# Attention probabilities as two fp16 halves, turned by DMA transposes instead of on TensorE

## The reference

```python
xn = ln(layernorm(x))                                  # per batch: 128 x 512
q, qx = ln(fp8(xn) @ wq.T), ln(fp8(xn) @ wqx.T)        # 16 heads each, d = 128
k, v = ln(fp8(xn) @ wk.T), fp8(xn) @ wv.T              # 8 groups, 2 heads share one
kx, vx = ln(cond @ w_kv_x[:1024].T), cond @ w_kv_x[1024:].T
def gqa(q, k, v):
    p = softmax(q @ k.T / sqrt(128))                   # 128 x 128 for each head
    return p @ v
cat = concat([gqa(q, k, v), gqa(qx, kx, vx)])          # 32 heads
x = x + fp8(cat / smooth) @ wproj.T * scale
```

## Time and profile before

| | |
|---|---|
| median of 3 runs | 3359.56 us (3355.34 to 3360.89) |
| the profiled execution | 3357.83 us |
| its span | 3356.0 us |
| mean granted TensorE clock | 0.948 of full |
| first residual written (L642) | at 194.7 us |
| last residual written | at 1156.4 us |

### The profile page before, as it was taken

One profiled execution on the slowest core, in us unless ns is written; L12 is line 12 of the kernel. 1 busy time (PEld: TensorE's weight loads), 2 busy tenths in 40 slices (PEclk: granted clock), 3 DMA queues, 4 the chain that ended last, 5 costly groups with the idle time before them and its releaser, 6 DMA issues. The chain is left out here.

```text
span 3356.0 us, 58815 instructions
## 1 busy us (share of the span) xinstructions
PE 2983.1 (89%) x17284; PEld 1767.7 (53%) x17285; DVE 1847.9 (55%) x5780; ACT 1650.6 (49%) x4374; POOL 1684.7 (50%) x2331
## 2 busy tenths in 40 slices
PE   4699999999999789999999995999999999734996
PEld 2366666666666545555555542555555555422663
DVE  4366666656665564434443363778878877421331
ACT  5577777777777533332333242555555555311332
POOL 6477667766776345534544453544444444241222
PEclk8799999999999989999999997999999999856998
DMA  7601101110110155544554473000000000217444
GB/s 239 216 30 42 38 28 35 41 38 28 35 44 29 67 178 156 152 134 138 154 155 140 129 221 68 17 26 19 19 25 19 19 25 14 65 74 273 85 83 105
DMA packets 202977, 285.48 MB, mean 85 GB/s; under 512 B 38721, under 2 KB 109633, under 8 KB 202817
## 3 DMA queue, kind: packets, MB, share of 16 engines
q1 hardware_dynamic: 140016, 204.89, 18.8%
q0 software_dynamic: 16640, 38.05, 5.6%
q10 hardware_dynamic: 46224, 41.36, 4.2%
HBM read 194.95 MB, written 93.50 MB: 86 GB/s over the span
## 5 line engine op out<-in xcount | busy, mean ns | idle before, releaser
L437 PE MATMUL a_mm<-a_w_hi,a_xq_hi 128*128 128x512 f16 x768 | 298.4, 389 | 64.0 <-POOL a_xq_lo L885 60.9
L601 DVE BATCH_NORM_STATS2 a_st<-a_mm 128x6 f32<-128x128 f32 x768 | 170.8, 285 | 318.8 <-PE a_mm L438 225.3
L750 ACT ACTIVATE a_nrm<-a_mm,a_sc_t 128x128 f32<-128x128 f32 x768 | 290.5, 473 | 105.9 <-POOL a_sc_t L903 105.7
L1646 POOL TENSOR_TENSOR e_st<-e_st,e_ws_tile 128x1024 f32<-128x1024 f32 x64 | 124.5, 1946 | 428.3 <-PE e_y L1402 417.5
L438 PE MATMUL a_mm<-a_w_hi,a_xq_lo 128*128 128x512 f16 x768 | 298.4, 389 | 0.0
L1535 DVE SCALAR_TENSOR_TENSOR e_hl<-e_ha,e_hh 128x512 f16<-128x512 f32 x128 | 88.5, 691 | 352.0 <-ACT e_hh L1440 351.6
L1440 ACT ACTIVATE e_hh<-e_ha 128x512 f16<-128x512 f32 x128 | 76.3, 596 | 415.3 <-PE e_ha L1387 413.7
L902 POOL TENSOR_TENSOR a_sc_t<-a_sc_t,a_mhalf 128x4 f32<-128x4 f32 x192 | 199.9, 1041 | 133.1 <-DVE a_sc_t L608 132.7
L1401 PE MATMUL e_y<-e_w2l,e_hh 128*128 128x512 f16 x640 | 242.9, 380 | 0.0
L1402 PE MATMUL e_y<-e_w2h,e_hl 128*128 128x512 f16 x640 | 242.9, 380 | 0.0
L1400 PE MATMUL e_y<-e_w2h,e_hh 128*128 128x512 f16 x640 | 242.9, 380 | 0.0
(11 more groups left out here) (357 smaller groups left out, 8653.7 us busy)
## 6 DMA issues: line engine op xcount, KB each, us to landing
e_st<-in_w SPq DMA_DIRECT2D x128, 512.0 KB, 4.1
disp<-a_empty SPq DMA_DIRECT2D x16, 781.5 KB, 4.1
e_st<-in_w1b SPq DMA_DIRECT2D x32, 352.0 KB, 3.1
e_xb<-disp ACTq DMA_DIRECT2D x41, 260.5 KB, 2.7
disp<-a_empty SPq DMA_DIRECT2D x4, 2605.0 KB, 21.5
e_xb<-disp SPq DMA_DIRECT2D x40, 260.5 KB, 4.3
a_cx<-in_ctxT SPq DMA_DIRECT2D x32, 256.0 KB, 3.1
a_stage<-in_wprojT SPq DMA_DIRECT2D x16, 512.0 KB, 5.0
```

What stands on the lines that cost most here:

```text
L437: pe.matmul(out, xq_hi[:, n, c, :], w_hi[:, t, c, :], start=(c == 0), stop=False)
L750: ins = act.activation(nrm[:, n % 2, i * P:(i + 1) * P], src[:, i * P:(i + 1) * P], ACT.Identity, bias=sc_t[:, n % 2, 3, i:i + 1], scale=s ...
```

## The change

Probabilities and values are kept as two fp16 parts each (high and low). ACT writes the high part of the probabilities, times PS = 1024, and DVE the rest; SP turns both with DMA transposes (128x512 each) into `pT`, and the value product is three fp16 products (high x high, high x low, low x high) in place of one in fp32. The values are split by ACT (`v_keep`) and DVE (`v_low`). `p_transpose` and `p_keep` are gone, `pv` and `out_project` come one slot later, `o_quant`, `final`, `store` and all `r_*` stages too, and the waits of the other users of PTB are changed accordingly. The factor PS is taken out in `rsm`.

```diff
-        vt = s.sb("vt", [P, 4, DM], F32)
+        vt = [s.sb(f"v{n}", [P, 4, DM], F16) for n in ("h", "l")]
         pr = s.sb("pr", [P, 2, DM], F32)
-        pT = s.sb("pT", [P, 2, DM], F32)
+        pq = [s.sb(f"pq{n}", [P, 2, DM], F16) for n in ("h", "l")]
+        pT = [s.sb(f"p{n}", [P, 2, DM], F16) for n in ("h", "l")]
...
+            def p_turn(b, a):                                         # SP
+                for half, done in ((0, "p_hi"), (1, "p_lo")):
+                    sp.wait_ge(sem[done], at(a, NA, b))
+                    if half == 0 and not (isinstance(b, int) and b == 0 and a < 2):
+                        sp.sem_inc(sem["turning"], 1)
+                        sp.wait_ge(sem["pv"], at(a - 2, NA, b))
+                    sp.sem_inc(sem["turning"], 1)
+                    sp.dma_start_transpose(pT[half][:, a % 2, :].rearrange("p (i t) -> p i t", t=P),
+                                           pq[half][:, a % 2, :]).then_inc(turned[half][a % 2], 16)
-            run_pipeline(sp, [("job", 0, ... weights ...), ("att", 5, residual), ("end", 10, store), ("in", 1, x_load)],
+            run_pipeline(sp, [("job", 0, ... weights ...), ("att", 4, p_turn), ("att", 5, residual),
+                              ("end", 11, store), ("in", 1, x_load)],
...
             def pv(b, a):                                             # PE
-                pe.wait_ge(sem["p_ok"], at(a, NA, b))
+                for half in range(2):
+                    pe.wait_ge(turned[half][a % 2], 16 * at(a // 2, NA // 2, b))
...
                 for i in range(2):
-                    mm = pe.matmul(OVB[:, i * 256:(i + 1) * 256], vt[...], pT[...], start=True, stop=True)
+                    pe.matmul(OVB[:, two], vh, ph, start=True, stop=False)
+                    pe.matmul(OVB[:, two], vh, pl, start=False, stop=False)
+                    mm = pe.matmul(OVB[:, two], vl, ph, start=False, stop=True)
-                              ("att", 3, p_transpose), ("att", 5, pv), ("att", 9, out_project), ("in", 6, x_transpose)],
+                              ("att", 6, pv), ("att", 10, out_project), ("in", 6, x_transpose)],
...
+            def v_low(b, t):                                          # DVE, waits for v_hi
+                    dve.scalar_tensor_tensor(out=vt[1][:, i, :], in0=MMB[BANK[t]][:], scalar=scal[:, col:col + 1],
+                                             in1=vt[0][:, i, :], op0=ALU.mult, op1=ALU.subtract).then_inc(sem["v_ok"], 1)
+            def p_low(b, a):
+                dve.wait_ge(sem["p_hi"], at(a, NA, b))
+                if not (isinstance(b, int) and b == 0 and a < 2):
+                    dve.wait_ge(turned[1][a % 2], 16 * at(a // 2 - 1, NA // 2, b))
+                dve.scalar_tensor_tensor(out=pq[1][:, a % 2, :], in0=pr[:, a % 2, :], scalar=PS, in1=pq[0][:, a % 2, :],
+                                         op0=ALU.mult, op1=ALU.subtract).then_inc(sem["p_lo"], 1)
-            run_pipeline(dve, [("att", 2, row_scale), ("att", 1, smax), ("att", 6, o_quant), ("end", 10, final), ("end", 10, r_stats),
-                               x_quants, ("job", 0, stats), ("job", 0, convert), ("in", 3, x_stats), ...
+            run_pipeline(dve, [("att", 2, row_scale), ("att", 1, smax), ("att", 3, p_low), ("att", 7, o_quant),
+                               ("end", 11, final), ("end", 11, r_stats),
+                               x_quants, ("job", 0, stats), ("job", 1, v_low), ("job", 0, convert), ("in", 3, x_stats), ...
...
             def exps(b, a):                                           # ACT
-                    act.wait_ge(sem["ptr"], at(a - 2, NA, b))
+                    act.wait_ge(sem["p_lo"], at(a - 2, NA, b))
-            def p_keep(b, a):
-                act.wait_ge(sem["ptr"], at(a, NA, b))
+            def p_high(b, a):
+                act.wait_ge(sem["pnorm"], at(a, NA, b))
                 if not (isinstance(b, int) and b == 0 and a < 2):
-                    act.wait_ge(sem["pv"], at(a - 2, NA, b))
-                act.activation(pT[:, a % 2, :], PTB[:], ACT.Copy).then_inc(sem["p_ok"], 1)
+                    act.wait_ge(turned[0][a % 2], 16 * at(a // 2 - 1, NA // 2, b))
+                act.activation(pq[0][:, a % 2, :], pr[:, a % 2, :], ACT.Copy, scale=PS).then_inc(sem["p_hi"], 1)
                ..., ("job", 3, q_keep), ("att", 1, exps), ("job", 1, normalise), ("job", 0, convert),
-                               ("att", 3, p_keep), ("job", 1, v_keep), ...
+                               ("att", 3, p_high), ("job", 1, v_keep), ...
```

More of the change, by code:

```diff
@@ L270, in layer0_attention @@
             "x_in", "c_in", "x_stat", "x_scal", "x_norm", "x_tr", "x_t", "y_act", "y_pool", "xq", "xq_ok", "cx_hi", "cx_lo",
-            "mm", "stat", "scal", "norm", "v_ok", "qtr", "q_ok",
-            "score", "max", "exp", "rinv", "pnorm", "ptr", "p_ok", "pv", "oy", "cq", "proj",
+            "mm", "stat", "scal", "norm", "v_hi", "v_ok", "qtr", "q_ok",
+            "score", "max", "exp", "rinv", "pnorm", "p_hi", "p_lo", "turning", "pv", "oy", "cq", "proj",
             "xres", "x1", "out", "filled", "disp_filled", "rconst", "r_stat", "r_scal", "r_norm", "r_tr", "r_t",
             "r_lgt", "r_lg", "r_max", "r_exp", "r_mask", "r_px", "r_pos", "r_slot")}
+        turned = [[s.sem(f"turned_{n}{i}") for i in range(2)] for n in ("h", "l")]
         staged = [s.sem(f"staged{i}") for i in range(NSTAGE + LENT)]
@@ L389, in store @@
                                  empty[:].unsqueeze(1).to_broadcast([P, FILL, RW])).then_inc(sem["filled"], 16)
-            run_pipeline(sp, [("job", 0, lambda b, t: weights(b, t + 1)), ("att", 5, residual), ("end", 10, store), ("in", 1, x_load)],
+            def p_turn(b, a):
[7 more added lines that the diff above has]
+                                           pq[half][:, a % 2, :]).then_inc(turned[half][a % 2], 16)
+            run_pipeline(sp, [("job", 0, lambda b, t: weights(b, t + 1)), ("att", 4, p_turn), ("att", 5, residual),
+                              ("end", 11, store), ("in", 1, x_load)],
                          NJ, SCORE_AT, head=HEAD)
@@ L401, in x_transpose @@
                 pe.wait_ge(sem["x_norm"], b + 1)
[L402 to L405, removed]
+                if isinstance(b, int) and b == 0:
                     pe.wait_ge(sem["small"], 16 * N_SMALL)
+                if not (isinstance(b, int) and b < 3):
+                    pe.wait_ge(sem["r_lg"], b - 2)
                 for c in range(KT):
@@ L461, in scores @@
                 mm.then_inc(sem["score"], 1)
[L463 to L479, removed]
             def pv(b, a):
@@ L487, in pv @@
                 for i in range(2):
-                    g = 2 * (a % 2) + i
-                    mm = pe.matmul(OVB[:, i * 256:(i + 1) * 256], vt[:, KV_OF[a], g * P:(g + 1) * P],
-                                   pT[:, a % 2, i * 256:(i + 1) * 256], start=True, stop=True)
+                    g, two = 2 * (a % 2) + i, slice(i * 256, (i + 1) * 256)
+                    vh, vl = (v[:, KV_OF[a], g * P:(g + 1) * P] for v in vt)
+                    ph, pl = (p[:, a % 2, two] for p in pT)
+                    pe.matmul(OVB[:, two], vh, ph, start=True, stop=False)
+                    pe.matmul(OVB[:, two], vh, pl, start=False, stop=False)
+                    mm = pe.matmul(OVB[:, two], vl, ph, start=False, stop=True)
                 mm.then_inc(sem["pv"], 1)
@@ L504, in out_project @@
                 mm.then_inc(sem["proj"], 1)
[L506 to L508 removed]
             def r_transpose(b, k):
[L511 to L512 removed]
+                if not (isinstance(b, int) and b == 0):
                     pe.wait_ge(sem["r_pos"], b)
@@ L690, in x_quant_of @@
                 return lambda b, k: x_quant(b, n)
-            run_pipeline(dve, [("att", 2, row_scale), ("att", 1, smax), ("att", 6, o_quant), ("end", 10, final), ("end", 10, r_stats),
-                               *(("in", at_, x_quant_of(n)) for n, at_ in enumerate(X_QUANT_AT)), ("job", 0, stats),
-                               ("job", 0, convert), ("in", 3, x_stats), ("end", 16, r_scores), ("end", 18, r_pick),
-                               ("end", 20, r_slots)], NJ, SCORE_AT, ch, head=HEAD)
+            run_pipeline(dve, [("att", 2, row_scale), ("att", 1, smax), ("att", 3, p_low), ("att", 7, o_quant),
+                               ("end", 11, final), ("end", 11, r_stats),
+                               *(("in", at_, x_quant_of(n)) for n, at_ in enumerate(X_QUANT_AT)), ("job", 0, stats), ("job", 1, v_low),
+                               ("job", 0, convert), ("in", 3, x_stats), ("end", 17, r_scores), ("end", 19, r_pick),
+                               ("end", 21, r_slots)], NJ, SCORE_AT, ch, head=HEAD)
         @block.scalar
@@ L817, in _ @@
                                ("in", 9, convert_at(-1)), ("job", 3, q_keep), ("att", 1, exps), ("job", 1, normalise), ("job", 0, convert),
-                               ("att", 3, p_keep), ("job", 1, v_keep), ("in", 4, x_norm), ("in", 6, x_back),
```

(7 more changed lines are left out.)

15 lines of the change are left out of this document (9 added, 6 removed).

## The result

| | before | after |
|---|---|---|
| median | 3357.45 us (3354.96 to 3360.89, 4 runs) | 3786.16 us (3784.7 to 3791.99, 4 runs) |
| ratio | | 1.1279, interval 1.126 to 1.1299 |
| profiled execution, its span | 3357.83, 3356.0 | 3791.99, 3790.2 |
| mean granted TensorE clock | 0.948 | 0.911 |

What follows compares the result with a forecast made beforehand. PE bounds the kernel before; a new loop of waits across DVE, POOL and ACT would bound it after. Batch 0 41 + 14 x 26.7 + drain 10 = 425 us on 3357.8: forecast 3785 us, range 3560 to 4000.

Steps and rivals of the forecast that it cites:

- The ring: First attention: p_low, stats, scales, normalise, exps, p_high wait in a circle; turns of 8.45 and 10.14 us plus extras; chance 0.72.
- PE's 5.2 us a batch are worth nothing: First attention: PE loses 0.65 us a head, 5.2 a batch, 83 in all, which become idle time.
- The ring's extras of slots 3 and 0: POOL's work ahead of scales: x_scale makes slot 3's turn grow by 5.3 us; pnorm, ctx_low, r_scale and others add 5.1 in slot 0.
- A batch of 93.7: First attention's batch after the change: 74.4 us of turns plus 19.3 of other work on the loop, 5.86 a slot.
- Batch 0, +41: First residual at 236 us against 194.7: p_turn(3) behind the fills, free at 160, then 13 slots, 76 us.
- A batch of 67.0 before: First attention in the kernel before: 14 batches from 193 to 1131 us, 67.0 us each, 4.19 a slot.
- The drain, +10: After the last slot 15: turns of 4.5 us without projections, 36 us against 26.
- The transposes, 1.6 us each, hidden: SP's 256 DMA transposes of 128 KB: 1.6 us each taken, two per turn hidden up to 5.9 us each.
- The rival in which they bind: Transposes take over from 5.9 us each; at 8 us, 128 us a batch and 4263 in all; chance 0.12.
- DVE's wait of 2 to 4 us at p_low: Sign in the profile after: DVE's longest wait is for ACT's p_high at p_low, 2 to 4 us, 120 times.
- PE at 65%: Sign in the profile after: PE's busy share in the first attention falls from 96% to near 65%.

Runs made afterwards that it cites:

- p_low_last: Kernel after with p_low moved behind stats and v_low of its slot in DVE's queue: 3431.73 us, ratio 1.0225.
- p_low_twice: Kernel after with DVE doing p_low twice in each step: 3877.9 us, ratio 1.156.
- pv_twice: Kernel after with PE making the six value products of each step twice: 3793.82 us, ratio 1.1307.
- fill_spread: Kernel after with the four 2605 KB fills issued one by one behind the transposes of steps 4 to 7 of batch 0: 3765.81 us.
- turn_twice: Kernel after with each transpose issued twice from batch 1 on, the first time into unused memory: 3797.16 us, ratio 1.1319.
- p_high_first: Kernel after with p_high moved ahead of exps and normalise of its slot in ACT's queue: 3573.03 us, ratio 1.0647.
- all_moves: Kernel after with p_low last, p_high first, x_scale, x_norm, ctx_low and r_scale later, and batch 0's big fills spread: 3288.54 us.

## Why the prediction was right, and where it was off

Point by point, by its own steps:

- **The ring** (chance 0.72): right, and shown from both sides. Order alone takes back 354 us (p_low_last); work in the ring costs its full length (p_low_twice), work beside it a tenth (pv_twice). Seven of the eight turns agree with their sums to 0.5 us.
- **PE's 5.2 us a batch are worth nothing**: right as a term (0.65 us a step, as summed), and right that it becomes idle time.
- **The ring's extras of slots 3 and 0**: right. Moving their pieces gave 107 us where these terms gave 114.
- **A batch of 93.7**: the mean over the 14 was 94.3, but two errors partly cancel in it. In the loop a batch takes 95.17, because one turn of eight has a `p_low` of 2.28 us in place of 0.69 (below). And the last batch prepares no next one: its turns lack x_scale, y_part and the rest, and it takes 1320.0-13x95.17 = 83 us. I had given it 93.7 like the others.
- **Batch 0, +41**: 43.9, and along the path described: SP issued the transpose behind the fills at 144.64, where it took the queue 10.36 us; PE stood still for it until 162.52 (160 forecast); from there to the first residual it is 76.1 us (76 forecast). What the change adds here is mostly the ring's slower slots and not the fills, which delay the kernel before by about as much (fill_spread, p_low_last).
- **A batch of 67.0 before**: half a microsecond too long. The kernel before writes its residual in slot 14 of the next batch (`final` stands at offset 10 behind slot 20), not in slot 15 as I had read it, so that the 938 us hold a slot more than 14 batches. From residual to residual it is 66.5. In the sum this is harmless: what the batches have too much, the drain has too little.
- **The drain, +10**: 6.1. The turns were 4.5, 5.0 and 3.5 us long by the starts of `p_low` (1566.14, 1570.61, 1575.58, 1579.04), close to the 4.5 taken; with 31.5 us in place of 36 the stretch as a whole was oversized. The 6.1 hold one slot more than before, and from the last residual but one to the last it is no longer than before (30.4 for 30.9).
- **The transposes, 1.6 us each, hidden**: hidden they were. They land in 2.4 us, between the taken value and the limit of 5.9. The rival in which they bind is out by turn_twice. The page "VectorE: DVE Perf Modes" of the Trainium skill (The three transpose paths) has 1309 ns for one 128x128 block of bf16. The trace does not bear out my estimate from that page, which added up four blocks to 5.2 us: one DMA of 128x512 fp16, four blocks, lands in 2.4 us and holds the queue for 1.19.
- **DVE's wait of 2 to 4 us at p_low**: undersized. It is 730.2 us in 128 times, 5.7 each. The length of a turn was right and its busy part on DVE too; I had not subtracted one from the other.
- **PE at 65%**: 72%. I counted PE's work at full clock. The granted clock in the stretch was 0.87 against 0.99 before (300 to 1000 us); L450 takes 433 ns in the mean with a median of 379 and 634 at most: part of the matmuls run at the lower of PE's two levels, 1.2 in place of 2.4 GHz (at 1555 us the projection's matmuls start 0.43 us apart, at 236 us 0.22). Since PE had time over, it cost little: 83 us of added work cost 7.7 (pv_twice).

The sum, 425 forecast and 434 measured in the profiled executions, is thus close partly by luck: some 11 us too many for the last batch and 4 for the drain stand against 13 x 1.5 = 20 too few in the loop and 3 in batch 0.

## What to carry to other kernels

Before a stage is put into a hand-written order, follow the queues in a circle: if engine A waits in slot t for B, B for C, and C for an instruction that stands behind A's waiting one, the loop's length is the new period, however idle each engine is. Busy shares of 50% on three engines with long waits that name each other are its mark in a profile, and the cheap test is to move the waiting stage behind what the others need. A change that frees the bound engine should be judged in an order in which nothing else stands on the path, and the kernel before with the same moves is the thing to compare it with.

## What the runs showed of the hardware

- **A DVE instruction three times as long.** `p_low` takes 691 to 693 ns, but once in each of batches 2 to 14 it takes 2.28 us, always in slot 11 (308.59, 403.65, 498.75, 593.91, 689.04 us and so on; 2.43 in the first). GpSimd is then a third of a microsecond into the first of two 128x512 pieces:

```profile
593.59 1.05 POOL L878 TENSOR_TENSOR a_xqs<-a_y,a_isc 128x512 f32<-128x512 f16 x1
594.59 1.05 POOL L887 TENSOR_TENSOR a_xq_hi<-a_y,a_isc 128x512 f16<-128x512 f16 x1
```

  `p_low` ends 0.55 us behind the end of the second piece (596.19 and 595.64), as if it stood still while both ran. In `p_high_first` it meets the first piece later, and each holds up the other: `p_low` takes 1.00 us and ends behind the first piece, and the second piece takes 1.49 us in place of 1.05:

```profile
541.49 1.04 POOL L878 TENSOR_TENSOR a_xqs<-a_y,a_isc 128x512 f32<-128x512 f16 x1
542.49 1.49 POOL L887 TENSOR_TENSOR a_xq_hi<-a_y,a_isc 128x512 f16<-128x512 f16 x1
...
542.07 1.00 DVE L615 SCALAR_TENSOR_TENSOR a_pql<-a_pr,a_pqh 128x512 f16<-128x512 f32 x1 [3.48 <-ACT a_pqh L795]
```

  GpSimd's being busy does not do it in general: in `all_moves` it is busy for 73% of the window, and `p_low` takes 682 ns in the mean of 102. There it meets only GpSimd's pieces of 128x4 and 128x1. In p_low_twice the mean of the first is 895 and of the second 692. What the two engines collide over is not shown here. It adds 1.6 us to the turn (13.43 for 11.8), some 20 us to the kernel after.
- **With more work PE had a higher granted clock.** With the products twice, the granted clock in 300 to 1300 us was 0.91 against 0.87, in an execution only 7.7 us longer:

```profile
300.00:1300.00 1000.00, 755.03 (x4184) 457.82 (x4185) 505.53 (x2017) 521.12 (x1574) 482.24 (x731) 0.91 0.19 48
```

  The added products, 5.2 us in a batch of 95, are 5.5% of the time, and PE's busy share rose by 3.5 points: it fits with part of what was added having come back by a faster clock of the rest. That the work in the gaps is what raised the clock is argued from this one pair.
- **The transpose's price on the DMA side.** The kernel after has 342243 packets for 202977 before, 139266 more with 256 transposes: 544 for each 128 KB, 241 bytes a packet. Yet it holds SP's queue for only 1.19 us.
